# Moving the chunk's maximum behind one or two depthwise taps in a fused graph-convolution and inverted-residual kernel

## The chip, the cores and the metric

The kernel runs on one core of one Trainium2 chip. The time is the device time of one execution in microseconds (us), the median of three runs; the profile is one more execution.

## The reference

The input is a batch of 16 images of 96 x 64 x 64. The first layer is a graph convolution over windows of 8 x 8 pixels:

```
y    = bn(conv1x1(x, fc1));  nodes = 64 pixels of a window, 96 channels
idx  = the 9 nearest nodes of each node (cosine distance, itself among them)
h    = gelu(bn(conv1x1([x_i, x_j - x_i], ew)))      # 192 channels, 9 neighbours
h    = max over the 9 neighbours
x1   = x + bn(conv1x1(h, fc2))
```

The second is an inverted residual block:

```
h = relu(bn(conv1x1(x1, w1)))         # 576 channels
h = relu(bn(depthwise3x3(h, wd)))     # 9 taps for each pixel
out = x1 + bn(conv1x1(h, w2))
```

## The kernel before, in words

An image has 64 windows, worked on in 32 pairs. The program of each engine is a loop over slots, one slot for each pair p of image b, written out for the images -1 and 0, looped for images 1 to 14 (two images to a pass of the loop, seven passes), and written out again for image 15 and a tail. All engines go through the same slots and meet only at semaphores. A chunk is four pairs (eight rows of the image), so an image has chunks 0 to 7. "Slot 17" below means p = 17.

The neighbours of pair P are found three slots ahead: TensorE makes the scores (L535, L537), VectorE takes the eight largest (`largest`, L902) and their indices (`indices`, L909) and makes a feature of them (`feature_a`, L919), ScalarE squares it (L739). TensorE transposes it (L546), expands it (L556), forms the values of the nodes (L570), and gathers them in three parts (`gather`, L583 and L586); ScalarE evaluates the gelu of each part (L765). VectorE reduces these over eight neighbours one slot later (`maxima`, L936), into `hid`. The ninth neighbour is the node itself: its gelu for a whole chunk lies in `gself`, and `join_self` (L945) takes the maximum of `hid` and `gself` for the whole chunk, in each slot with p % 4 == 0, for the chunk that ended with the pair before. It first waits until the last `maxima` of the chunk is done.

In the next slot (p % 4 == 1) TensorE multiplies that chunk with fc2 (L469, L471). This `fc2` job waits for `chunk_ready`, which the join raises. It stands early in TensorE's slot: behind `scores`, `gather` 0 and the transpose, and ahead of the expansion, `gather` 1, the w1 and w2 jobs, `values` and `gather` 2. TensorE works strictly in this order. ScalarE, too, has one order in a slot: gelu 0, the evacuations of the shared jobs (fc2 by L678), the one-hot matrices (L748), gelu 1, more evacuations, the values (L756), the square (L739, which waits for VectorE's `feature_a` of the same slot), gelu 2, and last, in slots with p % 8 == 0 and 1, the late first taps.

The depthwise convolution goes by strips of 16 rows in five groups of channels (0 to 4; group 4 has half the elements). ScalarE does tap 0 of each group (L775), VectorE the taps 1 to 8 (L958), 40 for a strip of eight slots: 5, 4, 5, 5, 5, 5, 6, 5 in the slots with p % 8 = 2, 3, 4, 5, 6, 7, 0, 1. Tap 1 of group 1, the second tap in a slot with p % 8 == 2, waits for tap 0 of group 1, which ScalarE does at the very end of the slot before. The lists `TAP_AT` and `TAP0_LATE` set this.

VectorE's order in a slot is: two taps, `largest`, (sometimes `normalise`), a tap, `indices`, a tap, `feature_a`, `maxima`, the join where p % 4 == 0, the remaining taps.

Of the kernel before, what the change touches and what calls it, by code (L numbers as in the profile page):

```python
# [13 lines left out]
PPC = PAIRS // CHUNKS  # L14
# [12 lines left out]
def valid(v, n):  # L27

    return not isinstance(v, int) or 0 <= v < n
# [34 lines left out]
def due_in(table, b, p):  # L64

    found = []
    for o in sorted(table, reverse=True):
        if (p - o) % SLOTS == 0:
            k = (p - o) // SLOTS - 2
            if valid(STRIPS * b + k, NSTRIPS):  # L70
                found.append((o, k % STRIPS, STRIPS * b + k, table[o]))
    return found
# [93 lines left out]
def tap_number(s, g, k):  # L166

    k -= 1
    return s * 5 * (TAPS - 1) + (2 * k + g if g < 2 else 2 * (TAPS - 1) + 3 * k + g - 2) + 1


def due(count):

    return not isinstance(count, int) or count > 0


def build(nc, x, p97, p128, rows97, consts, consts128, consts16, out):
# [3 lines left out]
    with ctx:  # L181
# [652 lines left out]
        def _(dve):  # L834
# [62 lines left out]
            def largest(P, p):  # L897

                if due(count := P + 1):
                    dve.wait_ge(score_ready, count)  # L900
                dve.sem_inc(dve_passed, 1)
                nc.vector.max(top8[:, p % 2, :], pscore[:, 0:NODES]).then_inc(top8_ready, 1)  # L902

            def indices(P, p):
                r = p % 2
                if due(count := P + 1):
                    dve.wait_ge(top8_ready, count)
                dve.sem_inc(dve_passed, 1)
                nc.vector.max_index(idx[:, r, :], top8[:, r, :], pscore[:, 0:NODES]).then_inc(idx_ready, 1)  # L909

            def feature_a(P, p):

                r = p % 2
                if due(count := P + 1):
                    dve.wait_ge(idx_ready, count)

                if due(count := P - 1):
                    dve.wait_ge(featT_ready, count)
                nc.vector.scalar_tensor_tensor(out=feat[:, r, 0:2 * KN].rearrange("p (win k) -> p win k", win=2),  # L919
                                               in0=idx[:, r, :].unsqueeze(1).to_broadcast([128, 2, KN]),  # L920
                                               scalar=-32.0, in1=maskw, op0=ALU.add, op1=ALU.mult).then_inc(a_ready, 1)

            def normalise(b, p, bi, c):
                dve.wait_ge(rows_loaded, 32 * (2 * bi + c // 4 + 1))

                if due(count := PPC * (CHUNKS * bi + c - 3)):
                    dve.wait_ge(score_ready, count)
                if due(count := CHUNKS * bi + c - 3):
                    dve.wait_ge(xs_ready, count)
                nc.vector.tensor_tensor(xn[:, c % 4, :], y[:, c, :], invb[:, c % 4, :], ALU.mult).then_inc(xn_ready, 1)  # L930

            def maxima(P, p):
                c, j, r = (p % PAIRS) // PPC, p % PPC, p % 2
                if due(count := 3 * P + 3):
                    dve.wait_ge(gelu_done, count)
                nc.vector.tensor_reduce(hid[:, c % 2, j, :, :], g[:, r], op=ALU.max, axis=AX.X).then_inc(hid_ready, 1)  # L936

            def join_self(b, p, bc, c):

                if due(count := PAIRS * bc + PPC * (c + 1)):  # L940
                    dve.wait_ge(hid_ready, count)
                fb, fp = when(b, p, 3 if c % 2 else 1)
                dve.wait_ge(misc_evac, job_at(fb, fp, "self_full", c))
                dve.sem_inc(dve_passed, 1)
                nc.vector.tensor_tensor(hid[:, c % 2], hid[:, c % 2], gself[:, c % 2], ALU.max).then_inc(chunk_ready, 1)  # L945

            def tap(s, sp_, gr, k):

                dy, dx = k // 3, k % 3
                n = STRIP if gr < FULL else STRIP // 2  # L950
                src = hpad[:, gr, dy:dy + n, dx:dx + W]
                dst = acc[:, sp_, gr, 0:n * W].rearrange("p (row col) -> p row col", col=W)
                wk = wd[:, gr, k:k + 1]
                if k == 1:
                    dve.wait_ge(tap0_done, 5 * s + gr + 1)
                else:
                    dve.wait_ge(tap_done, tap_number(s, gr, k - 1))
                nc.vector.scalar_tensor_tensor(out=dst, in0=src, scalar=wk, in1=dst, op0=ALU.mult,  # L958
                                               op1=ALU.add).then_inc(tap_done, 1)

            def image(b, p0, p1):
                for p in range(p0, p1):
                    P = PAIRS * b + p
                    taps = [(s, t % 2, gr, k) for _, t, s, entries in due_in(TAP_AT, b, p) for gr, k in entries]
                    new = valid(P + 3, NPAIRS)
                    h = 1 if p < 16 else 0
                    bi = b if h else b + 1

                    for a in taps[0:2]:
                        tap(*a)  # L970
                    if new:
                        largest(P + 3, p + 3)
                    if p % 16 in XN_AT and valid(bi, B):
                        normalise(b, p, bi, 4 * h + XN_AT[p % 16])
                    for a in taps[2:3]:
                        tap(*a)
                    if new:
                        indices(P + 3, p + 3)
                    for a in taps[3:4]:
                        tap(*a)  # L980
                    if new:
                        feature_a(P + 3, p + 3)
                    if valid(P - 1, NPAIRS):
                        maxima(P - 1, p - 1)
                    if p % PPC == 0:
                        bc, c = (b, p // PPC - 1) if p else (b - 1, CHUNKS - 1)
                        if valid(bc, B):
                            join_self(b, p, bc, c)
                    for a in taps[4:]:
                        tap(*a)  # L990

            image_loop(dve, image, TAIL)


# [83 lines left out]
```

## Time and profile before

| | |
|---|---|
| median of three runs | 4279.18 us (4278.34 to 4279.40) |
| the profiled execution | 4282.92 us, its span 4281.2 us |
| busy in the span | VectorE 96%, TensorE 93%, ScalarE 83%, GpSimd 13% |
| mean granted TensorE clock | 0.984 of full speed |
| DMA | 31 GB/s in the mean |

Matmuls are pipelined and their ends are modelled, so that 93% is an upper figure. In a timeline row the first number is the start and the second the time until the last of the merged instructions ends; VectorE's instructions overlap by about 0.08 us, so that the distance of two starts is the better price. Idle time in brackets is that of the engine just ahead of the row, with what ended it.

### The profile page before, as it was taken

To read this page: it belongs to the slowest core of one execution; us is meant where nothing else is said; L and a number is where in the kernel's file an instruction comes from. 1 tells how busy PE (TensorE), PEld (TensorE's weight loads), DVE (VectorE), ACT (ScalarE), POOL (GpSimd) and SP (SyncE) were. 2 spreads that over 40 slices of the span, in tenths; PEclk is the share of its full clock that TensorE was granted. 3 is DMA by queue.
4 is the path that set the end of the run, shared out by engine and by line. 5 is a ranking of instruction groups with operands and counts; after the bars stand their busy time and mean duration, and the time that the engine had idled before them with its cause. 6 is when DMAs were issued, how large, how long until landed. Compare 5 with 4: busy or idle time off the path is not lost.

```text
span 4281.2 us, 78057 instructions
## 1 busy us (share of the span) xinstructions
PE 3989.6 (93%) x23360; PEld 2150.9 (50%) x23360; DVE 4095.6 (96%) x5418; ACT 3563.9 (83%) x6885; POOL 554.0 (13%) x548
## 2 busy tenths in 40 slices
PE   5999999999999999999999999999999999999984
PEld 2445555555554555555555555555555555555442
DVE  2599999999999999999999999999999999999998
ACT  3888888888888888888888888888888888888873
POOL 0011111011111011111011111011111111111100
PEclk9999999999999999999999999999999999999997
DMA  1111121111111111120111111111120111210111
GB/s 48 23 31 33 25 46 18 33 38 32 34 31 31 27 38 33 25 46 14 36 38 24 42 29 31 29 35 33 29 44 16 37 35 25 44 27 18 29 23 22
DMA packets 52971, 133.76 MB, mean 31 GB/s; under 512 B 7778, under 2 KB 9058, under 8 KB 46372
## 3 DMA queue, kind: packets, MB, share of 16 engines
q0 software_dynamic: 28672, 50.35, 8.2%
q1 hardware_dynamic: 23876, 78.22, 7.0%
q8 instruction: 211, 3.46, 0.3%
q14 instruction: 212, 1.74, 0.1%
HBM read 77.68 MB, written 25.69 MB: 24 GB/s over the span
## 4 chain that ended last, share of the span: by engine, by line
PE 46%; DVE 27%; issue 18%; ACT 6%; DVEq 1%; DMA 0%; SPq 0%; ACTq 0%; POOL 0%; POOLq 0%
DVE acc L958 19%; PE pg L583 12%; PE pmisc L511 6%; PE pmisc L495 5%; DVE hid L936 5%; PE pg L586 5%; PE pvu L570 5%; PE pmisc L447 2%; PE pmisc L454 2%; ACT MV L748 2%; PE pvu L556 2%; PE pmisc L513 1%; DVE idx L909 1%; PE pmisc L469 1%; PE pmisc L471 1%
## 5 line engine op out<-in xcount | busy, mean ns | idle before, releaser
L958 DVE SCALAR_TENSOR_TENSOR acc<-hpad,w,acc 128x1024 f32<-128x1024 f32 (+1 forms) x2560 | 2921.7, 1176 | 22.3 <-ACT acc L775 14.7
L583 PE MATMUL pg<-MV,VU 128*128 128x512 f32 x2048 | 1153.4, 645 | 80.0 <-ACT VU L756 67.1
L765 ACT ACTIVATE g<-pg 128x512 f32<-128x512 f32 x1536 | 910.6, 593 | 148.3 <-PE pg L583 59.0
L936 DVE TENSOR_REDUCE hid<-g 128x192 f32<-128x1536 f32 x512 | 894.0, 1746 | 0.0
L748 ACT ACTIVATE MV<-pvu,cst 64x512 f32<-64x512 f32 x1024 | 695.2, 679 | 13.0 <-PE pvu L556 5.0
L495 PE MATMUL pmisc<-x,w 96*128 96x384 f32 (+1 forms) x1536 | 567.1, 488 | 18.4 <-ACT hpad L695 17.5
L586 PE MATMUL pg<-MV,VU 128*64 128x512 f32 x2048 | 527.5, 592 | 0.0
L511 PE MATMUL pmisc<-acc,w 128*96 128x256 f32 x2048 | 494.9, 385 | 30.5 <-ACT acc L782 30.5
L695 ACT ACTIVATE hpad<-pmisc,sh,sc 128x384 f32<-128x384 f32 (+1 forms) x768 | 475.8, 660 | 24.1 <-DVE acc L958 11.3
L570 PE MATMUL pvu<-wVU,y 97*64 97x192 f32 x4096 | 446.6, 339 | 16.3 <-ACT MV L748 16.3
L511 PEld LDWEIGHTS pmisc<-acc,w 128*96 128x96 f32 x2048 | 331.3, 164 | 213.6 <-issue 109.7
L495 PEld LDWEIGHTS pmisc<-x,w 96*128 96x128 f32 x1536 | 287.8, 193 | 291.3 <-issue 163.0
L570 PEld LDWEIGHTS pvu<-wVU,y 97*64 97x64 f32 x4096 | 248.6, 136 | 286.3 <-issue 135.9
L782 ACT ACTIVATE acc<-acc,shd,scd 128x1024 f32<-128x1024 f32 (+1 forms) x320 | 360.3, 1147 | 31.2 <-DVE acc L958 31.2
L583 PEld LDWEIGHTS pg<-MV,VU 128*128 128x128 f32 x2048 | 310.9, 192 | 132.0 <-issue 113.3
L775 ACT ACTIVATE acc<-hpad,w 128x1024 f32<-128x1024 f32 (+1 forms) x320 | 339.5, 1062 | 0.1
L535 PEld LDWEIGHTS pscore<-xn,xs 97*64 97x64 f32 x2048 | 143.0, 137 | 346.9 <-issue 272.0
L370 POOL DMA_DIRECT2D x<-in_x_dram x128 | 102.0, 797 | 1538.4 <-ACT x L678 1530.6
L412 POOL COPY xs<-xn 96x512 f32<-96x512 f32 x128 | 159.8, 1249 | 1080.6 <-DVE xn L930 1080.6
L756 ACT ACTIVATE VU<-pvu 128x384 f32<-128x384 f32 x512 | 249.7, 488 | 55.0 <-PE pvu L570 53.1
L556 PEld LDWEIGHTS pvu<-featT,c 128*128 128x128 f16 x4096 | 180.8, 99 | 225.6 <-issue 186.4
L379 POOL DMA_DIRECT2D res<-x x128 | 103.9, 812 | 985.8 <-ACT res L726 929.9
(96 smaller groups left out, 4007.1 us busy)
## 6 DMA issues: line engine op xcount, KB each, us to landing
xin<-in_x_dram SPq DMA_DIRECT2D x32, 768.0 KB, 5.8
invb<-rows_dram SPq DMA_DIRECT2D x32, 768.0 KB
x<-in_x_dram POOLq DMA_DIRECT2D x128, 192.0 KB, 3.6
res<-x POOLq DMA_DIRECT2D x128, 192.0 KB, 3.5
out_dram<-res SPq DMA_DIRECT2D x128, 192.0 KB, 2.1
g<-in_consts_dram SPq DMA_DIRECT2D x1, 640.0 KB
w<-in_p_dram SPq DMA_DIRECT2D x1, 618.5 KB
rows_dram<-norm_rows SPq DMA_DIRECT2D x32, 16.0 KB, 1.4
```

The costliest lines, as they stand in the source:

```text
L495: last = nc.tensor.matmul(ps[:, o:o + (hi - lo) * W], w1T[:, gr * 128:(gr + 1) * 128], x1[:, lo:hi, :], start=True, stop=True)
L511: nc.tensor.matmul(ps[0:C, 0:4 * W], w2T[:, gr, :], acc[:, par, gr, q * 4 * W:(q + 1) * 4 * W], start=(gr == 0), stop=False)
L570: last = nc.tensor.matmul(pvu[h:h + 64, O * w:O * (w + 1)], nodes, wVU[:, k, :], start=True, stop=True)
L583: last = nc.tensor.matmul(ps[:, :], VU[:, r, part, 0:ONE128], cols[part], start=True, stop=True)
L586: last = nc.tensor.matmul(ps[64 * w:64 * w + 64, :], VU[:, r, w, ONE128:O], cols[w], start=True, stop=True)
L695: nc.scalar.activation(hpad[:, gr, r0:r1, 1:W + 1], ps[:, o:o + (r1 - r0) * W].rearrange("p (row col) -> p row col", col=W), ACT.Relu, bia ...
L748: last = nc.scalar.activation(MV[h:h + 64, p % 2, w, :].rearrange("p (n k) -> p n k", k=KN), pone[h:h + 64, :, :].rearrange("p k n -> p n ...
L765: nc.scalar.activation(g[:, p % 2, part, :, :], pg[(3 * p + part) % 2][:, :].rearrange("p (n k) -> p n k", k=KN), ACT.Gelu).then_inc(gelu_ ...
L775: nc.scalar.activation(acc[:, t % 2, gr, 0:rows * W].rearrange("p (row col) -> p row col", col=W), hpad[:, gr, 0:rows, 0:W], ACT.Copy, sca ...
L782: nc.scalar.activation(acc[:, par, gr, 0:n], acc[:, par, gr, 0:n], ACT.Relu, bias=shd[:, gr:gr + 1], scale=scd[:, gr:gr + 1]).then_inc(rel ...
L936: nc.vector.tensor_reduce(hid[:, c % 2, j, :, :], g[:, r], op=ALU.max, axis=AX.X).then_inc(hid_ready, 1)
L958: nc.vector.scalar_tensor_tensor(out=dst, in0=src, scalar=wk, in1=dst, op0=ALU.mult, op1=ALU.add).then_inc(tap_done, 1)
```

## The change

In slots with p % 4 == 0 the join is issued behind the remaining taps in place of ahead of them. The cut of the list of taps becomes a variable, `last`.

```diff
+                    last = min(len(taps) - 1, 4) if p % PPC == 0 else 4
 ...
-                    for a in taps[3:4]:
+                    for a in taps[3:last]:
                         tap(*a)
                     if new:
                         feature_a(P + 3, p + 3)
                     if valid(P - 1, NPAIRS):
                         maxima(P - 1, p - 1)
+                    for a in taps[last:]:
+                        tap(*a)
                     if p % PPC == 0:
                         bc, c = (b, p // PPC - 1) if p else (b - 1, CHUNKS - 1)
                         if valid(bc, B):
                             join_self(b, p, bc, c)
-                    for a in taps[4:]:
-                        tap(*a)
```

## Rows read from the trace of the kernel before

**Rows 1.** Busy time in one pass of the loop: PE, PEld, DVE, ACT, POOL, clock, DMA.

```profile
1626.90:2142.40 515.50, 493.72 (x2921) 267.11 (x2921) 509.11 (x672) 444.43 (x861) 70.28 (x68) 0.99 0.16 32
```

**Rows 2.** Who waited for whom in the whole span: us, times, longest us.

```profile
DVE top L902 <- PE pscore L537: 60.5, 21, 5.7
PE pmisc L469 <- DVE hid L945: 49.7, 28, 7.1
```

**Rows 3.** VectorE's timeline: a join in slot 0, and slot 1 behind it.

```profile
2108.64 1.74 DVE L936 TENSOR_REDUCE hid<-g 128x192 f32<-128x1536 f32 x1
2110.61 0.96 DVE L945 TENSOR_TENSOR hid<-hid,gself 128x768 f32<-128x768 f32 x1 [0.23 <-DVE hid L936]
2111.49 3.80 DVE L958 SCALAR_TENSOR_TENSOR acc<-hpad,w,acc 128x512 f32<-128x512 f32 x4
...
2116.74 1.27 DVE L958 SCALAR_TENSOR_TENSOR acc<-hpad,w,acc 128x1024 f32<-128x1024 f32 x1
2117.93 0.17 DVE L919 SCALAR_TENSOR_TENSOR feat<-idx,cst 128x16 f16<-128x16 uint32 x1
2118.01 1.75 DVE L936 TENSOR_REDUCE hid<-g 128x192 f32<-128x1536 f32 x1
2119.68 1.94 DVE L958 SCALAR_TENSOR_TENSOR acc<-hpad,w,acc 128x512 f32<-128x512 f32 x2
```

**Rows 4.** TensorE's timeline: the fc2 job in slot 1.

```profile
2111.72 1.07 PE L469 MATMUL pmisc<-hid,w 128*96 128x256 f32 x4 [1.65 <-DVE hid L945]
```

**Rows 5.** ScalarE in slot 1, then VectorE's first two taps in slot 2.

```profile
2113.69 0.68 ACT L678 ACTIVATE x<-pmisc,l0sc 96x512 f32<-96x512 f32 x1 [2.50 <-PE pmisc L471]
...
2118.13 0.22 ACT L739 ACTIVATE feat<-feat 128x16 f16<-128x16 f16 x1 [0.23 <-DVE feat L919]
...
2118.73 1.14 ACT L775 ACTIVATE acc<-hpad,w 128x1024 f32<-128x1024 f32 x1
...
2120.34 2.48 DVE L958 SCALAR_TENSOR_TENSOR acc<-hpad,w,acc 128x1024 f32<-128x1024 f32 x2
```

**Rows 6.** The same pair of rows around slots 10 and 26.

```profile
1665.79 1.14 ACT L775 ACTIVATE acc<-hpad,w 128x1024 f32<-128x1024 f32 x1
...
1667.39 2.48 DVE L958 SCALAR_TENSOR_TENSOR acc<-hpad,w,acc 128x1024 f32<-128x1024 f32 x2
...
2053.88 1.17 ACT L775 ACTIVATE acc<-hpad,w 128x1024 f32<-128x1024 f32 x1
...
2054.74 2.48 DVE L958 SCALAR_TENSOR_TENSOR acc<-hpad,w,acc 128x1024 f32<-128x1024 f32 x2
```

**Rows 7.** Timelines at the end of a loop pass: TensorE's restart, VectorE in slot 2.

```profile
1845.51 0.48 PE L535 MATMUL pscore<-xn,xs 97*64 97x64 f32 x4 [3.47 <-issue]
...
1864.98 1.28 DVE L958 SCALAR_TENSOR_TENSOR acc<-hpad,w,acc 128x1024 f32<-128x1024 f32 x1 [1.18 <-ACT acc L775]
```

**Rows 8.** Windows behind pauses of TensorE (columns as in rows 1; clock third from last).

```profile
813.60:820.30 6.70, 6.66 (x22) 3.30 (x23) 6.42 (x9) 2.93 (x6) 0.00 (x0) 0.50 0.02 5
...
3394.10:3397.40 3.30, 3.30 (x14) 1.69 (x13) 3.30 (x7) 1.31 (x4) 0.00 (x0) 0.50 0.01 2
2240.40:2243.70 3.30, 3.30 (x14) 1.72 (x13) 3.30 (x6) 0.47 (x1) 0.00 (x0) 0.50 0.26 71
...
3530.60:3533.90 3.30, 3.30 (x13) 1.60 (x12) 3.30 (x5) 0.14 (x1) 0.00 (x0) 0.50 0.20 60
952.20:955.60 3.40, 3.37 (x18) 1.98 (x19) 3.40 (x4) 1.39 (x3) 0.00 (x0) 1.00 0.20 58
```

**Rows 9.** ScalarE and VectorE behind the fall of the clock at 2240 us.

```profile
2248.17 1.14 ACT L775 ACTIVATE acc<-hpad,w 128x1024 f32<-128x1024 f32 x1
...
2248.51 1.28 DVE L958 SCALAR_TENSOR_TENSOR acc<-hpad,w,acc 128x1024 f32<-128x1024 f32 x1
...
2312.52 1.29 DVE L958 SCALAR_TENSOR_TENSOR acc<-hpad,w,acc 128x1024 f32<-128x1024 f32 x1 [0.16 <-ACT acc L775]
```

**Rows 10.** VectorE in the tail, behind the last join.

```profile
4174.41 86.03 DVE L958 SCALAR_TENSOR_TENSOR acc<-hpad,w,acc 128x1024 f32<-128x1024 f32 x79 [0.27 <-ACT acc L775]
```

## The prediction, made before the kernel was run

> **What bounds the kernel.** I read the page first: VectorE 96% busy, TensorE 93%, ScalarE 83%. The windows of one loop pass sharpen this [rows 1]: VectorE is busy for 509.1 of 515.5 us, TensorE for 493.7. So VectorE sets the pace with 6.4 us of idle time in a pass, and TensorE, 4% idle, follows closely. The list of waits shows the rest [rows 2]: VectorE waited for scores only in 21 slots, all before 181 us, when no strip of taps had begun; and TensorE waited 28 times for the join, 49.7 us in all. By the timeline of each of the 128 joins those waits are all on joins of odd chunks (slots 0, 8, 16, 24 of VectorE, served in slots 1, 9, 17, 25 of TensorE). The even chunks' joins are ready 1.8 us or more before TensorE comes. The waits are long for chunk 3 (1.8 us) and, away from a loop's end, chunk 7 (1.65 us) [rows 4]; for chunk 1 TensorE mostly comes 0.2 us after the join, for chunk 5 1.1 us after.
>
> **What the change does.** `last` is 4 wherever a strip's taps are due in such a slot, since 5 (slots 4, 12, 20, 28) or 6 (0, 8, 16, 24) taps stand there and never 4 or fewer. So no tap that stood ahead of `maxima` moves. The join alone moves behind one whole tap in the first kind of slot, and behind a half and a whole tap in the second. No DMA, no instruction and no semaphore is added; SP and GpSimd are not passed. In the first image's slots 4 to 16 there are no taps, so 4 of 128 joins stay as they are.
>
> **The gain.** Before, the join stands right behind the `maxima` whose end it must see. From the start of that reduction to the join 1.97 us pass (2108.64 to 2110.61), from the same reduction to a tap 1.67 us (2118.01 to 2119.68) [rows 3]. The difference, 0.30 us, is bare VectorE time. Behind a tap of 1.19 us (2116.74 to 2117.93) the reduction is long done when the join's turn comes, and the tap hides both the wait and the two extra instructions of the sequencer. Bounds: 0 to 0.30 us for each join; I take 0.30, as every other VectorE instruction behind a tap starts without a gap. That is 16 x 0.30 = 4.8 us in a pass, 37 us for 124 joins.
>
> The Trainium skill, "VectorE: DVE Perf Modes", section "The DRAIN you can't avoid", says the opposite: copies with a semaphore after each took as long as copies with one at the end, so a semaphore between them costs nothing. By that rule the gain is 0 and the sum below would be 37 us higher. The bracket of 0.23 us ahead of this join, with the reduction named as its cause, contradicts it [rows 3].
>
> **The cost on the chain.** The join ends later by what passes it: 1.19 us in even chunks, and 0.66 (2119.68 to 2120.34) + 1.19 = 1.85 us in odd ones [rows 3, 5], counted against VectorE's own end of slot. Even chunks have 1.8 us of room or more and lose nothing. In odd ones TensorE starts fc2 1.85 us later against VectorE, and everything behind fc2 in its strict order follows, ScalarE too: its fc2 evacuation waited 2.50 us for TensorE [rows 5]. What is late next is tap 0 of group 1, ScalarE's last work in that slot, for which VectorE's second tap of the next slot waits. Its room before:
> - slots 2 and 18: 2118.73 + 1.14 = 2119.87 against 2120.34 + 1.19 = 2121.53, so 1.66 us [rows 5];
> - slot 10: by the same sum 1666.93 against 1668.58, 1.65 us; slot 26: 2055.05 against 2055.93, 0.88 us [rows 6];
> - slots 2 behind a loop's end: none, VectorE already idles 1.18 us there, as TensorE restarted after a pause of 3.47 us [rows 7]; and slot 10 of that image, too, had 0.03 us left.
>
> How much lateness reaches those taps is seen where the clock fell at 2240 us: TensorE ran at 0.50 for 3.4 us [rows 8], so lost 1.7 us. At slot 18 the room had shrunk to 2249.70 - 2249.31 = 0.39 us, so 1.27 us had arrived; at slot 26 the 0.88 us were gone and 0.16 us of idle time added, so 1.0 us [rows 9]. Some 0.4 and 0.7 us wear off. The gain itself eats room as well: 0.3 us at each join between. So, in us for one pass:
> - slots 2 and 18: 1.85 - 0.4 = 1.45 < 1.63: nothing.
> - slot 26, twice: 1.85 - 0.7 + 0.6 - 0.85 = 0.9 each, 1.8.
> - slot 10, twice: about 0.5 each (1.85 - 0.4 + 0.6 - 1.6 = 0.45 in one image, the two joins' 0.6 against no room in the other), 1.0.
> - slot 2 behind the loop's end: no room; what TensorE is still late there, 1.1 + 0.3 less its own short waits, 0.8.
>
> Together 3.6 against the gain of 4.8: without more, -1.2 us in a pass, -8 us in seven.
>
> **The clock.** TensorE's wait for the join grows. For chunk 3 it was 1.8 us and gets 1.85 us more, less the 0.3 to 0.5 us by which TensorE comes later itself: about 3.2 us. For chunk 7 away from a loop's end about 2.7 us. The granted clock stood at 0.50 behind all six pauses of 3.5 to 4.1 us at the loop's ends, for 3.4 us or 6.8 us, and behind four of the 21 waits for the join of 1.6 to 1.8 us between 300 and 4100 us; behind the others it stayed at 1.00 (0.50 and 1.00 are the levels of 1.2 and 2.4 GHz) [rows 8]. Before, a fall behind chunk 3 cost VectorE next to nothing, since the room at slot 18 took it. Now that room is used up, and of each fall 1.3 us [rows 9] goes into VectorE's time. Bounds for the share of long waits that are followed by a fall: 4/21 (waits of 1.8 us) to 6/6 (3.5 us and more); being nearer to the second I take 0.87. Three long waits in a pass x 0.87 x 1.3 = 3.4 us.
>
> The Trainium skill, "TensorE: Matmul & The Clock Gate", section "HAM oscillation — how this bites in real kernels", tells of a loop whose recurring wait throttles TensorE anew each time, at a price of half the throttled time. By that price a fall would cost 1.7 us, and the three waits 4.4 us in place of 3.4.
>
> **The sum.** A pass: -4.8 + 3.6 + 3.4 = +2.2 us, seven passes +15. Image 0 has four moved joins (-1.0), and its chunk 5, where TensorE waits already, costs its full 1.85: +1. Image 15 has seven (-2) and three waits that lengthen by the same amount, with falls: +1.5. The last join starts the tail's chain; VectorE idled 0.27 us at its end [rows 10], so the tail ends 1.85 - 0.30 = 1.55 us later. Together +4. The sum is +19.5 us: the profiled execution of 4282.9 us would be 4302.4, and as it stood 3.7 us above the median of 4279.2, I predict 4299 us.
>
> **Rivals.**
> - *The longer waits bring no more falls of the clock than before.* Then the sum is -8 + 4 - 1 = -5 us, 4274 us. For it: 17 of 21 waits of 1.7 us were followed by none. Against it: the waits become nearly twice as long. Chance 0.24.
> - *The gain comes whole, and TensorE's lateness vanishes in its own 4% of idle time* (the other side). One mechanism: ScalarE's last tap 0 keeps its place because VectorE's feature, not TensorE, releases it; the 0.23 us bracket ahead of its square shows such a release [rows 5]. It decides if more than 1.5 us of lateness wears off before slot 26. Then -37 + 1.5: 4244 us. Against it, 1.0 us of 1.7 arrived there [rows 9]. Chance 0.12.
> - *VectorE gains nothing behind the tap* (the skill's rule, or a new gap ahead of the join). The costs stay, partly smaller since no room is eaten: -0 + 3.6/2 + 3.4 a pass, +36 + 4: about 4320 us. Chance 0.05.
> - *The change does nothing*, because `last` equals the old cut: true of the taps, not of the join. No chance of its own.
>
> **How the numbers follow.** The likeliest case, with falls, has 0.59; its own range is 4286 to 4318, from half the falls to all of them at 1.7 us. The range of 8 in 10 must take in the case without falls: 4264 to 4320. Within 0.2% (8.6 us, about what these measurements can tell from no change) lie most of the case without falls and a little of the likeliest: 0.22. Faster by more: 0.17; slower by more: 0.61.
>
> **What would show it.** Right: no idle time ahead of L945; VectorE's busy time unchanged; TensorE's wait for L945 at 100 us or more in place of 49.7; waits ahead of L469 near 3 us in slots 1 and 17; idle time ahead of L958 ended by L775 at 30 us or more in place of 14.7; a mean granted clock below 0.984, near 0.975. Wrong: idle time ahead of L945 as before (the gain), L469 waiting no longer than before (the shift), L958 starting without gaps in slots 2, 10 and 26 (room), or a clock of 0.984 (the falls).

## The result, and the profile after

The changed kernel is slower: 4309.3 us in the median of six runs (4306.5 to 4318.2) against 4278.8 us (4277.0 to 4279.4) of the kernel before, a ratio of 1.0074 with a 95% interval of 1.0061 to 1.0087. That is +30.5 us where +20 us was forecast. The profiled execution, of 4306.5 us, is the fastest of the six.

The page of the changed kernel, first and third line:

```profile
span 4304.7 us, 78057 instructions
...
PE 4000.1 (93%) x23360; PEld 2161.9 (50%) x23360; DVE 4089.1 (95%) x5418; ACT 3555.6 (83%) x6885; POOL 595.0 (14%) x548
```

No instruction was added, VectorE is busy for 6.5 us less than before, and the span is 23.5 us longer. So it is waiting that was added. The windows of one pass of the loop, over the same two images as [rows 1]:

```profile
1636.10:2154.90 518.80, 496.77 (x2924) 269.13 (x2922) 508.45 (x673) 443.38 (x861) 75.88 (x68) 0.98 0.16 32
```

A pass takes 518.8 us in place of 515.5; VectorE's idle time in it has grown from 6.4 to 10.4 us. The list of waits says where (us, times, longest us). First two rows of the kernel before that [rows 2] doesn't have:

```profile
DVE hid L945 <- DVE hid L936: 22.4, 97, 0.3
DVE acc L958 <- ACT acc L775: 14.7, 15, 4.9
```

Then the changed kernel:

```profile
PE pmisc L469 <- DVE hid L945: 93.7, 28, 8.4
DVE acc L958 <- ACT acc L775: 74.4, 57, 4.9
DVE top L902 <- PE pscore L537: 60.3, 21, 5.5
...
DVE hid L945 <- DVE hid L936: 0.7, 4, 0.2
```

The last line is the gain: all idle time ahead of the join was 29.8 us before (22.4 us of it put down to the reduction), and it is 0.7 us now, ahead of the four joins at the start that have no tap between reduction and join. The first is the shift: TensorE waits for the join as often as before and almost twice as long. At 93.7 us it falls short of the 100 us that the prediction gave as a sign. The second is the loss: VectorE waits for ScalarE's tap 0 in 57 places for 74.4 us, where there were 15 for 14.7 us. The wait for scores is that of the start, as it was.

VectorE's timeline at the join of slot 0, to be laid beside [rows 3]:

```profile
2119.25 1.74 DVE L936 TENSOR_REDUCE hid<-g 128x192 f32<-128x1536 f32 x1
2120.91 1.93 DVE L958 SCALAR_TENSOR_TENSOR acc<-hpad,w,acc 128x512 f32<-128x512 f32 x2
2122.77 0.95 DVE L945 TENSOR_TENSOR hid<-hid,gself 128x768 f32<-128x768 f32 x1
2123.64 1.94 DVE L958 SCALAR_TENSOR_TENSOR acc<-hpad,w,acc 128x1024 f32<-128x1024 f32 x2
```

The bracket ahead of L945 is gone. TensorE in the same place [rows 4], and for chunk 3 of the next image:

```profile
2120.48 0.19 PE L546 MATMUL pfeat<-c,feat 128*128 128x64 f16 x1
2123.86 0.71 PE L469 MATMUL pmisc<-hid,w 128*96 128x256 f32 x1 [3.18 <-DVE hid L945]
...
2249.50 0.19 PE L546 MATMUL pfeat<-c,feat 128*128 128x64 f16 x1
2253.00 1.48 PE L469 MATMUL pmisc<-hid,w 128*96 128x256 f32 x3 [3.31 <-DVE hid L945]
```

The wait for the same chunk 3 in the kernel before:

```profile
2239.89 1.59 PE L469 MATMUL pmisc<-hid,w 128*96 128x256 f32 x4 [1.78 <-DVE hid L945]
```

1.65 us became 3.18, and 1.78 became 3.31. What the clock did behind the second of these, and behind a wait of 3.19 us at 2644 us, is in the windows (clock third from last):

```profile
2249.80:2253.00 3.20, 0.00 (x0) 0.03 (x1) 3.20 (x5) 1.14 (x3) 0.38 (x1) 1.00 0.46 61
2253.20:2256.50 3.30, 3.30 (x8) 1.44 (x8) 3.30 (x7) 0.00 (x0) 0.00 (x0) 0.50 0.22 65
2644.20:2647.50 3.30, 3.30 (x18) 1.88 (x19) 3.30 (x7) 1.39 (x3) 0.00 (x0) 1.00 0.07 23
```

TensorE did nothing for 3.2 us, then ran at 1.2 GHz for 3.4 us in one case and at 2.4 GHz in the other. Of the 24 waits for the join of 3.2 to 3.4 us between 300 and 4100 us, 19 went with a fall, which began between 1.3 us ahead of their end and 0.5 us behind it. The falls have two lengths: 15 lasted 3.4 us and four 6.8 us. One of the four, and VectorE behind it (slots 17 and 18 of another image):

```profile
2512.60:2519.30 6.70, 6.08 (x17) 3.23 (x18) 6.70 (x10) 1.99 (x4) 0.79 (x1) 0.50 0.10 29
```

```profile
2524.00 1.28 DVE L958 SCALAR_TENSOR_TENSOR acc<-hpad,w,acc 128x1024 f32<-128x1024 f32 x1 [2.74 <-ACT acc L775]
```

And VectorE, with ScalarE's row of the same moment, behind the wait at 2253 us (slots 17 and 18), in slot 26, and in slot 10:

```profile
2256.66 0.68 ACT L678 ACTIVATE x<-pmisc,l0sc 96x512 f32<-96x512 f32 x1 [5.72 <-PE pmisc L471]
...
2261.33 1.17 ACT L775 ACTIVATE acc<-hpad,w 128x1024 f32<-128x1024 f32 x1
...
2262.53 1.28 DVE L958 SCALAR_TENSOR_TENSOR acc<-hpad,w,acc 128x1024 f32<-128x1024 f32 x1 [1.50 <-ACT acc L775]
...
2325.89 1.28 DVE L958 SCALAR_TENSOR_TENSOR acc<-hpad,w,acc 128x1024 f32<-128x1024 f32 x1 [1.10 <-ACT acc L775]
...
1677.09 1.28 DVE L958 SCALAR_TENSOR_TENSOR acc<-hpad,w,acc 128x1024 f32<-128x1024 f32 x1 [0.72 <-ACT acc L775]
```

The tap in slot 18 starts 0.03 us after tap 0 ends (2261.33 + 1.17 = 2262.50). In [rows 5] and [rows 6] the same taps had 1.66, 0.88 and 1.65 us of room.

In the loop's slots 18 and in the slots 2 away from a loop's end, this wait of VectorE follows the clock, wait by wait. Behind each of the 17 long waits of TensorE with a fall VectorE idles, and behind the four without one it doesn't.

### The profile page after: what moved, and what is told of

The parts are those of the page before. It is cut to its first block, busy times and chain, and to the rows that moved or that the text cites. A ratio compares the mean times of both kernels' runs of the same rounds, so it can differ in the third digit from the quotient of the medians.

```text
span 4304.7 us, 78057 instructions
## 1 busy us (share of the span) xinstructions
PE 4000.1 (93%) x23360; PEld 2161.9 (50%) x23360; DVE 4089.1 (95%) x5418; ACT 3555.6 (83%) x6885; POOL 595.0 (14%) x548
## 4 chain that ended last, share of the span: by engine, by line
PE 61%; DVE 16%; issue 13%; ACT 9%; DVEq 0%; DMA 0%; SPq 0%; ACTq 0%; POOL 0%; POOLq 0%
PE pg L583 16%; DVE acc L958 10%; PE pmisc L495 8%; PE pg L586 7%; PE pvu L570 6%; PE pmisc L511 6%; DVE hid L936 3%; PE pmisc L469 2%; ACT MV L748 2%; PE pmisc L454 2%; PE pmisc L471 2%; PE pvu L556 2%; PE pmisc L477 2%; PE pmisc L447 2%; PE pmisc L513 2%
## 5 line engine op out<-in xcount | busy, mean ns | idle before, releaser
L958 DVE SCALAR_TENSOR_TENSOR acc<-hpad,w,acc 128x1024 f32<-128x1024 f32 (+1 forms) x2560 | 2928.6, 1172 | 81.4 <-ACT acc L775 74.4
L469 PE MATMUL pmisc<-hid,w 128*96 128x256 f32 x512 | 152.2, 424 | 93.7 <-DVE hid L945 93.7
```

## The experiments

Each kernel ran next to the kernel before on the same chip. Medians in us; the kernel before had 4279.8, 4279.4 and 4280.1 in the three groups (e1 to e4, e5 to e8, and e9 to e11; 9, 27 and 7 runs).

| kernel | median | ratio, 95% interval |
|---|---|---|
| changed kernel | 4309.3 | 1.0074 (1.0061 to 1.0087) |
| e1_even, join moved in even chunks alone | 4261.8 | 0.9960 (0.9946 to 0.9973) |
| e2_odd, join moved in odd chunks alone | 4317.4 | 1.0085 (1.0071 to 1.0099) |
| e3_short, in odd chunks behind the half tap alone | 4264.8 | 0.9964 (0.9950 to 0.9977) |
| e4_early_max, maxima earlier, join not later | 4241.6 | 0.9912 (0.9897 to 0.9928) |
| e5_fc2_last, changed kernel, fc2 behind w1 and w2 | 4242.7 | 0.9914 (0.9900 to 0.9928) |
| e6_fill, changed kernel, idle time filled for chunk 3 | 4281.6 | 1.0008 (0.9998 to 1.0017) |
| e7_fc2_last_b, kernel before, fc2 behind w1 and w2 | 4283.1 | 1.0007 (0.9998 to 1.0016) |
| e8_tap0, changed kernel, tap 0 ahead of gelu 2 | 4289.4 | 1.0020 (1.0011 to 1.0029) |
| e9_both, e4's order of VectorE and e5's of TensorE | 4238.9 | 0.9906 (0.9890 to 0.9923) |

### The two halves of the change: e1_even and e2_odd

```diff
-                    for a in taps[last:]:
+                    cut = 4 if p % SLOTS == 0 else len(taps)
+                    for a in taps[last:max(last, cut)]:
                         tap(*a)
                     if p % PPC == 0:
...
                             join_self(b, p, bc, c)
+                    for a in taps[max(last, cut):]:
+                        tap(*a)
```

This is e1_even, where `cut` leaves the join of the slots 0, 8, 16 and 24 ahead of its taps; in e2_odd the two values of `cut` are exchanged.

> The join is moved only in slots with p % 8 == 4 (even chunks), behind one tap; in slots 0, 8, 16, 24 it stands where it stood before. Theory (each moved join gives VectorE 0.30 us, and the cost comes only through fc2 of the odd chunks): 60 joins x 0.30 = 18 us gained and nothing paid, so about 4261 us; TensorE's wait for the join stays near 50 us, falls of the clock stay at about 19. Rival (a join behind a tap saves nothing, or the change costs something of its own at each join): 4279 us or more.

> The other half: the join is moved only in slots 0, 8, 16, 24, behind its two taps. Theory (all of the cost sits here): slower than the changed kernel, since half of the gain is missing. Of the missing 18 us some comes back because less room is eaten ahead of slots 10 and 26 (4 x 0.3 us in a pass, 8 us), so about 4309 + 18 - 8 = 4319 us; TensorE's waits for the join about 94 us as in the changed kernel. Rival (the costs are spread over all joins): about half way between the kernel before and the changed one, 4294 us.

Measured: 4261.8 us and 4317.4 us, where the theory had 4261 and 4319. The rows of the list of waits, of e1_even and then of e2_odd:

```profile
PE pmisc L469 <- DVE hid L945: 49.5, 28, 6.8
DVE acc L958 <- ACT acc L775: 16.1, 18, 4.9
DVE hid L945 <- DVE hid L936: 13.5, 59, 0.3
```

```profile
PE pmisc L469 <- DVE hid L945: 94.5, 28, 8.7
DVE acc L958 <- ACT acc L775: 67.5, 56, 4.9
DVE hid L945 <- DVE hid L936: 13.4, 58, 0.2
```

Each half keeps half of the reduction's wait; only the odd half has the long waits of TensorE. The even half is worth 18.0 us and costs next to nothing (16.1 us of waits for tap 0 against 14.7). It covers 62 joins in the trace, not the 60 of the expectation, so a join is worth 0.29 us. So the cost is not one of the join's place as such: it sits in the odd chunks, and the rival of costs spread evenly (4294 us) falls. The two halves, -18.0 and +37.6 us, add up to 19.6 us and not to the 30.5 us of the whole change. Most of the difference is the room which the gain itself eats: the slots 10 have 4.4 us of idle time ended by tap 0 in the loop of e2_odd and 9.6 us in that of the changed kernel, the slots 26 12.5 and 15.5 us.

### A shorter delay: e3_short

```diff
-                    for a in taps[last:]:
+                    cut = 5
+                    for a in taps[last:cut]:
                         tap(*a)
...
                             join_self(b, p, bc, c)
+                    for a in taps[cut:]:
+                        tap(*a)
```

> As the changed kernel, but in slots 0, 8, 16, 24 the join stands between the two taps: behind the half one (0.66 us), ahead of the whole one. Theory (the price is the time by which fc2 starts later, and it is paid only beyond the room of about 0.9 and 1.6 us): the full gain of 37 us; lost are about 1 us in a pass where there is no room (behind a loop's end), 0.3 to 0.6 us in slots 26 and 10, and a few more falls of the clock as the waits go from 1.8 to 2.2 us: 4250 to 4262 us. Rival (the price goes in proportion to the delay, 0.66/1.85 of 68 us): 4279 - 37 + 24 = 4266 us. If it is the place behind any tap that costs: 4309 us.

Measured: 4264.8 us, 2.8 us above my range and next to the proportional rival's 4266. VectorE's waits for tap 0 were 33.5 us in 39 places, TensorE's for the join 61.5 us. By the timeline the slots 26 had 11.2 us of them in the loop's seven passes (0.8 us each) and the slots 10 had 5.7 us (0.4 us each), where I had expected 0.3 to 0.6, while slots 2 away from a loop's end and slots 18 had 2.4 us in all. In the slots 2 behind a loop's end, where I had expected about 1 us more in a pass, the 7.5 us are those of the kernel before. That is the pattern of a room used up at some places and not at others; the time alone does not tell it from a price in proportion.

### The gain without the delay: e4_early_max

```diff
                         indices(P + 3, p + 3)
+                    if valid(P - 1, NPAIRS) and p % PPC == 0:
+                        maxima(P - 1, p - 1)
+                        if new:
+                            feature_a(P + 3, p + 3)
                     for a in taps[3:4]:
                         tap(*a)
-                    if new:
+                    if new and not (valid(P - 1, NPAIRS) and p % PPC == 0):
                         feature_a(P + 3, p + 3)
-                    if valid(P - 1, NPAIRS):
+                    if valid(P - 1, NPAIRS) and p % PPC != 0:
                         maxima(P - 1, p - 1)
```

> The kernel before, but in slots with p % 4 == 0 the order is indices, maxima, feature_a, tap, join, remaining taps: the tap that stood ahead of maxima now lies between maxima and the join. So the join's own wait is covered as in the changed kernel, while fc2 is released no later than before (0.3 us earlier). Theory: the whole gain and none of the cost, 4279 - 37 = 4242 us, TensorE's wait for the join about 50 us or less. Rival (feature_a comes 0.5 us later in these slots and holds up the chain through ScalarE, or gain and cost can't be parted): 4255 us or more.

Measured: 4241.6 us. VectorE's timeline at such a join (slot 12):

```profile
1671.34 0.22 DVE L909 FIND_INDEX8 idx<-top,pscore 128x8 uint32<-128x64 f32 x1
1671.48 1.73 DVE L936 TENSOR_REDUCE hid<-g 128x192 f32<-128x1536 f32 x1
1673.13 0.16 DVE L919 SCALAR_TENSOR_TENSOR feat<-idx,cst 128x16 f16<-128x16 uint32 x1
1673.22 1.27 DVE L958 SCALAR_TENSOR_TENSOR acc<-hpad,w,acc 128x1024 f32<-128x1024 f32 x1
1674.41 0.94 DVE L945 TENSOR_TENSOR hid<-hid,gself 128x768 f32<-128x768 f32 x1
```

A tap covers the join's wait here as in the changed kernel, and as many instructions lie ahead of the join as before the change. Gain and cost can be parted: 38 us less than before, 68 us less than the changed kernel. The 38 us are not a clean measure of the gain, though: VectorE's busy time is 17.3 us less than before, in the changed kernel 6.5 us, as here `feature_a` and the reductions stand in another order too.

### TensorE's place of the wait: e5_fc2_last and e7_fc2_last_b

```diff
-ORDER = ('ssq', 'fc1', 'inv', 'self_full', 'self_half', 'fc2', 'w1', 'w2')
+ORDER = ('ssq', 'fc1', 'inv', 'self_full', 'self_half', 'w1', 'w2', 'fc2')
```

> The changed kernel with the shared jobs sorted so that fc2 comes behind w1 and w2 in its slot, on TensorE and ScalarE alike. TensorE then has 2 us or more of other work ahead of the wait for the join. Theory (the whole cost is TensorE's early wait for the join): the waits for L945 nearly vanish, no falls of the clock outside the loop's ends, idle time of VectorE ahead of L958 small, and the gain of 37 us stands: 4240 to 4255 us. Rival (the cost lies in VectorE's new order itself): near 4309 us.

> The kernel before with fc2 behind w1 and w2. Theory (VectorE sets the pace before, TensorE's waits for the join cost nothing there): within 5 us of 4279, at most a few us less at the loop's ends. Rival (TensorE's wait for the join costs time before as well): 4260 us or less.

Measured: 4242.7 us with VectorE's order of the changed kernel, 4283.1 us with that of the kernel before (its expectation was within 5 us of 4279). TensorE's timeline for chunk 3 in e5_fc2_last:

```profile
2218.89 0.81 PE L495 MATMUL pmisc<-x,w 96*128 96x384 f32 x2
2220.45 1.08 PE L469 MATMUL pmisc<-hid,w 128*96 128x256 f32 x4 [0.75 <-DVE hid L945]
```

VectorE's order is that of the slow kernel, to the instruction, and the loss is gone; so it came through the early place of fc2. `ORDER` sorts the jobs of TensorE and of ScalarE alike, so this run does not part TensorE's wait for the join from ScalarE's wait for fc2 (5.72 us in the row above). And this early place cost nothing before the change, since taking it away there gains nothing: VectorE waits for tap 0 for 12.4 us in e7_fc2_last_b and for 14.7 us in the kernel before. That kernel has more falls of the clock than the kernel before, 26 against 19, and 14 of them came behind pauses of 0.8 to 1.6 us that `indices` ended. One of these, with the clock until it fell and behind that:

```profile
3018.81 0.34 PE L535 MATMUL pscore<-xn,xs 97*64 97x64 f32 x4 [1.01 <-DVE idx L909]
```

```profile
3018.90:3021.10 2.20, 2.10 (x15) 1.13 (x15) 2.20 (x3) 1.04 (x3) 0.00 (x0) 1.00 0.62 89
3021.20:3027.90 6.70, 6.70 (x23) 3.76 (x23) 6.70 (x11) 4.70 (x11) 0.00 (x0) 0.50 0.00 1
```

Why the clock fell there stays open.

### The clock: e6_fill

```diff
                     bc, c = job[1:]
+                    if c == 3:
+                        for _ in range(2):
+                            nc.tensor.matmul(ps[0:C, :], fc1T, w97[0:C, 0:512], start=True, stop=True)
                     if due(count := CHUNKS * bc + c + 1):
                         pe.wait_ge(chunk_ready, count)
```

> The changed kernel, with two matmuls of 96 x 512 on constants issued to the free bank ahead of the wait for the join, for chunk 3 alone, where TensorE idles 3.3 us in every image. They do no useful work (the bank is overwritten by fc2) and should cost nothing, as 1.9 us of work lies in 3.3 us of idle time; what they change is that TensorE's pause shrinks to about 1.4 us. Theory (each fall of the clock behind such a wait costs 1.3 us of VectorE's time): the 13 or 14 falls behind chunk 3's waits are gone, 17 to 18 us less than the changed kernel: about 4292 us, idle time at slot 18 gone. Rival (the falls cost nothing, the delay of fc2 alone does): 4309 us.

Measured: 4281.6 us, 27.7 us less than the changed kernel, for work that is thrown away. TensorE's timeline for chunk 3 (behind the edit this kernel's lines are numbered 3 higher, L472 is fc2; the first row is the two added matmuls), and the clock behind it:

```profile
2239.62 1.94 PE L466 MATMUL pmisc<-w 96*96 96x512 f32 x4
2242.99 1.10 PE L472 MATMUL pmisc<-hid,w 128*96 128x256 f32 x4 [1.43 <-DVE hid L948]
```

```profile
2243.20:2246.50 3.30, 3.30 (x18) 1.86 (x18) 3.30 (x7) 1.49 (x3) 0.10 (x1) 1.00 0.22 65
```

The fc2 job is released at the same point of VectorE's order as in the changed kernel; only TensorE's pause is shorter, 1.43 us for 3.31. In this profile no wait for chunk 3 is followed by a fall, and VectorE has no idle time ended by tap 0 in any slot 18, where the changed kernel's loop has 21.7 us behind 13 waits. I had expected 17 to 18 us less time, at 1.3 us for each fall. That price fits the ten falls of 3.4 us, which cost 1.36 us each in the mean (1.16 to 1.50); but three falls lasted 6.8 us and cost 2.7 us each. The rest is that the falls behind chunk 7's waits also became rare (one of nine waits of 3.2 us, six of nine in the profile of the changed kernel), though these waits were not filled; the 5.2 us of idle time in slots 2 away from a loop's end are gone as well. Why they became rare no run here settles.

### VectorE's wait: e8_tap0

```diff
+                    for o, t, s, groups in due_in(TAP0_LATE, b, p):
+                        for gr in groups:
+                            if gr == 1:
+                                tap0(b, p, o, t, gr)
                     if valid(P, NPAIRS):
                         gelu(P, p, 2)
                     for o, t, s, groups in due_in(TAP0_LATE, b, p):
                         for gr in groups:
-                            tap0(b, p, o, t, gr)
+                            if gr != 1:
+                                tap0(b, p, o, t, gr)
```

> The changed kernel, with ScalarE doing tap 0 of group 1 ahead of gelu 2 in its slot in place of behind it, some 0.5 us earlier, or more where gelu 2 waits for TensorE. Theory (VectorE's loss is its wait for this tap 0, 74 us in 57 times, most of them 0.7 to 1.8 us): each wait shrinks by 0.5 us or more, 25 to 40 us less: 4270 to 4284 us. Rival (the loss is TensorE's pace as such and the wait at tap 1 only where it shows): the idle time moves to another place (largest or maxima) and the time stays near 4309 us.

Measured: 4289.4 us (4279.4 to 4294.3), 19.9 us less than the changed kernel and 5 us above the range. Its list of waits (L963 is the tap, L907 `largest`):

```profile
DVE top L907 <- PE pscore L537: 67.5, 39, 5.5
DVE acc L963 <- ACT acc L775: 46.5, 55, 4.4
```

The wait for tap 0 shrank by 27.9 us, some 0.5 us in each place; 7.2 us came back as waits for scores in 18 more slots, 24 and 23 above all. Both theories are partly right: tap 0 is where TensorE's lateness reaches VectorE first, and a few tenths of a microsecond behind it stands the next place.

### Both orders: e9_both

The edits of e4_early_max and e5_fc2_last together, on the kernel before.

> The early maxima of e4_early_max and fc2 behind w1 and w2 together. Theory: both remove the same cost and both have the gain, so they don't add up: 4238 to 4243 us. Rival (each removes something of its own): 4225 us or less.

Measured: 4238.9 us (4236.3 to 4241.3). They don't add up, as each already takes away the same cost. It is the fastest kernel of the study, by 2.8 us over e4_early_max and in another group of runs, so not clearly.

### The spread: e10_after_again and e11_after_third

The changed kernel, profiled twice more, one execution each.

> The changed kernel once more, a second profile. Theory: its time spreads more than the kernel's before (4306 to 4318 us) because the number of pauses of 3.2 us that are followed by a fall of the clock differs from run to run; each of them costs 1.3 to 1.7 us. So the difference of this profiled time to 4306.5 us is 1.3 to 1.7 us times the difference to the 19 falls behind such waits of that profile. Rival: the number of falls is the same and the time differs for another reason.

> A third profile of the changed kernel, for the same comparison as the second.

Measured, the falls counted over the same 24 waits: 4306.5 us with 19 falls (the first profile), 4307.3 us with 20 (e11_after_third), 4313.6 us with 21 (e10_after_again). VectorE's wait for tap 0 in the slowest, e10_after_again:

```profile
DVE acc L958 <- ACT acc L775: 80.0, 59, 4.9
```

The order is as expected and 5.6 of the 7.1 us more lie in that row, but 7.1 us for two falls is more than twice 1.7, so the expectation misses the size. The number of falls is the wrong measure, as they have two lengths. Of 3.4 and of 6.8 us there were 15 and 4, 17 and 3, and 15 and 6: 78.5, 78.5 and 92.1 us at 0.50. So the profile with one fall more than the first had as much low clock and nearly its time, and the slowest had 13.6 us more of it. Three profiles fit this; they are too few to show that it is all of the spread.

## Why the prediction was right

**The gain** was sized right: 0.30 us for a join was forecast. e1_even measures it alone, 0.29 us (18.0 us for 62 joins). The sum for 124 joins was 37 us. Of these, 29.1 us are the idle time ahead of the join (29.8 to 0.7 us), and VectorE's busy time fell by another 6.5 us: an instruction that needn't see the reduction's end overlaps it by 0.08 us. The prediction set against this the Trainium skill, "VectorE: DVE Perf Modes", section "The DRAIN you can't avoid", by which a semaphore after each copy costs nothing extra. The measurement is against that rule for this join. The page tells of a row of copies, and here the instruction waits for the end of a reduction right ahead of it.

**The shift** was right for chunk 3, forecast at 3.2 us and measured at 3.31. For chunk 7 it was forecast at 2.7 us and is 3.18. **The room** was right in place and nearly in size. Summed over the timeline of the loop, as idle time ended by tap 0, less that of before, in us for a pass (the last row is the pass itself, by the seven in the mean):

| | forecast | measured |
|---|---|---|
| slots 26 | 1.8 | 2.1 |
| slots 10 | 1.0 | 1.3 |
| slot 2 behind a loop's end | 0.8 | 0.6 |
| slots 18 and the other slot 2 (the clock) | 3.4 | 3.85 |
| a pass in all, with the gain | +2.2 | +3.1 |

**The clock** was the term that decided the sign, and it came out at 3.85 us a pass where 3.4 was forecast. Its two factors were both off, and the errors partly made up for each other, by luck. The share of long waits with a fall was put at 0.87 and was 17 of 21 in these slots, 0.81. The price was put at 1.3 us and was 1.58 in the mean. For a fall of 3.4 us it was right: 14 such falls cost 1.34 us each. What the sum left out were falls of 6.8 us, three of them at 2.7 us each, although [rows 8] has one at a loop's end.

The Trainium skill, "TensorE: Matmul & The Clock Gate", section "HAM oscillation — how this bites in real kernels", prices a fall at half of its throttled time. By that, falls of 3.4 and 6.8 us would cost 1.7 and 3.4 us. The trace does not reach it: VectorE lost 1.34 and 2.7 us. For some of the falls part of the low clock lay in TensorE's wait itself (0.7 to 0.8 us of each of the three long ones).

Without the falls behind chunk 3 (and, by luck, most of those behind chunk 7) the kernel takes 4281.6 us: so of the 68 us between the best order and the changed kernel some 28 are the clock's, and about 40 are left for the delay of fc2. My rival without falls had 4274 us; it was 8 us too low.

**The ends.** For the two outer images and the tail I took +4 us. The seven passes take 3607.4 us before and 3629.2 us now, cut at slot 9, and what these 21.8 us leave of the 23.5 us is 1.7 us. The tail's idle time grew from 0.27 [rows 10] to 1.27 us:

```profile
4198.30 2.48 DVE L958 SCALAR_TENSOR_TENSOR acc<-hpad,w,acc 128x1024 f32<-128x1024 f32 x2 [1.27 <-ACT acc L775]
```

**Where the 10 us are.** Against the profiled executions I forecast 4302.4 us and 4306.5 came: the passes were sized 6.4 us too low (15.4 against 21.8) and the ends 2.3 us too high. The larger part, 6.6 us, is in the step to the median: I took off 3.7 us, by which the profile before stood above its median, while the profile after stands 2.9 us below its own. The changed kernel spreads over 12 us in six runs, the kernel before over 2 us in six and 8.5 us in the 27 runs of another group, so a single profile is a weak hold for such a correction.

Of the rivals, the vanishing of lateness in TensorE's idle time falls with slots 26 (1.10 us of wait), the missing gain with e1_even, and that of no more falls than before with the 19 falls behind 24 waits.

## What to carry to other kernels

An instruction that another engine waits for early in its strict order has a price for being late that no list of busy shares shows: look up how much room stands behind that wait, place by place, and what the pause does to TensorE's clock. To cover an engine's wait for its own last result, move the producer forward and leave the consumer where it is (e4_early_max), or move the other engine's wait behind work that it has anyway (e5_fc2_last); either turned a loss of 30 us into a gain of 37. And an engine that is idle for 4% of the time has not 4% of slack: here 1.85 us of lateness in one slot of eight was more than it had.

## What the runs showed of the hardware

- Two useless matmuls, 1.94 us together, in each wait of 3.3 us for chunk 3 made the kernel 28 us faster. TensorE's granted clock then stayed at 2.4 GHz (1.00), where it had fallen to 1.2 GHz (0.50) behind 13 such waits of the loop, ten times for 3.4 us and three times for 6.8 us.
- With no room left, a fall of 3.4 us cost VectorE 1.34 us in the mean of 14, and one of 6.8 us 2.7 us in each of three.
- A wait's length alone doesn't decide whether the clock falls: waits of 3.18 to 3.19 us of one kind were followed by a fall in six of nine cases in one kernel and in one of nine in another; and in e7_fc2_last_b 14 falls came 2 to 3 us behind the end of pauses of 0.8 to 1.6 us.
- VectorE, behind a reduction whose end it must see, starts 0.32 us later than behind one whose end it needn't see: in the kernel before, 1.98 us after the reduction's start in the mean of 128 joins, 1.66 us in that of 372 taps. In time, e1_even gives 0.29 us for a join.
